# Two attention layers with one pipelined schedule: value products in pairs of quads, four probability buffers, heads divided group by group, token tiles finished in pairs

## The reference, cut to what matters

```python
def layer_a(x):                      # 16 heads of 16
    q, k, v = split(x @ Wqkv)
    q, k = rope(q), rope(k)
    q, k = q / |q|, k / |k|          # 1e-6 under the root
    a = softmax(q k^T / sqrt(16))
    return (a v) @ Wo + bo
x = layernorm(x + layer_a(x))
h = layernorm(x) * ln1_w + ln1_b
x = x + msa(h)                       # 16 heads, no rope, logits not bounded
y = layernorm(x) * ln2_w + ln2_b
x = x + expert(y)                    # 8 experts, the one with the largest gate logit
return layernorm(x + ...)            # hidden 1024, tanh gelu
```

## Time and profile before

| | us |
|---|---|
| median of 3 runs | 1553.11 (1550.62 to 1556.96) |
| the profiled execution | 1552.78, its span 1551.0 |
| busy: TensorE | 1334.5 (86%) |
| ScalarE | 959.3 (62%) |
| VectorE | 817.5 (53%) |
| GpSimd | 330.8 (21%) |

### The profile page before, as it was taken

How to read it: one execution, slowest core, us unless ns; L and a number is a source line. 1 busy time by engine, 2 the same in 40 slices (tenths; PEclk the granted TensorE clock), 3 DMA queues, 4 the chain that set the end, 5 groups by cost and what they waited for, 6 DMA issues and landing times. The chain is left out here.

```text
span 1551.0 us, 21330 instructions
## 1 busy us (share of the span) xinstructions
PE 1334.5 (86%) x7238; PEld 690.7 (45%) x7238; DVE 817.5 (53%) x1911; ACT 959.3 (62%) x1809; POOL 330.8 (21%) x337
## 2 busy tenths in 40 slices
PE   3599898898997889899999999999983499999994
PEld 1223333333332324343434343434332389899893
DVE  4232563544634267777777777777751334333341
ACT  0176776776777756666666666666670167777774
POOL 5122232322322202122212121212112201111110
PEclk9599999999999989999999999999995599999997
DMA  6212413313223312122312121212238211211113
GB/s 165 95 40 74 133 35 102 101 46 127 65 75 128 100 42 73 63 69 66 85 60 83 56 82 56 82 56 83 96 110 279 87 35 53 58 52 52 52 55 129
DMA packets 104010, 127.89 MB, mean 82 GB/s; under 512 B 7680, under 2 KB 91520, under 8 KB 103776
## 3 DMA queue, kind: packets, MB, share of 16 engines
q1 hardware_dynamic: 72080, 79.45, 16.4%
q10 hardware_dynamic: 27392, 33.56, 6.5%
q0 software_dynamic: 4432, 13.52, 2.7%
HBM read 51.51 MB, written 28.46 MB: 52 GB/s over the span
## 5 line engine op out<-in xcount | busy, mean ns | idle before, releaser
L670 ACT ACTIVATE w_space<-bank 128x512 f32<-128x512 f32 x1024 | 569.3, 600 | 296.9 <-PE bank L451 287.9
L451 PE MATMUL bank<-w_space 96*128 96x512 bf16 (+1 forms) x1024 | 366.2, 387 | 35.3 <-ACT w_space L670 21.3
L853 DVE TENSOR_REDUCE negm<-bank 128x1 f32<-128x512 f32 x512 | 327.4, 683 | 103.2 <-PE bank L478 100.2
L465 PE MATMUL bank<-w_space 128*32 128x512 f32 x2048 | 280.3, 620 | 11.4 <-ACT w_space L670 8.3
L478 PE MATMUL bank<-w_space 96*128 96x512 bf16 x512 | 198.9, 389 | 28.7 <-ACT neg_T L683 11.3
L451 PEld LDWEIGHTS bank<-w_space 96*128 96x128 bf16 (+1 forms) x1024 | 98.5, 100 | 230.0 <-ACT w_space L670 122.4
L478 PEld LDWEIGHTS bank<-w_space 96*128 96x128 bf16 x512 | 49.7, 97 | 215.4 <-DVE negm L853 104.0
L643 PE MATMUL bank<-w_space,work_space 128*128 x624 | 141.6, 380 | 0.0
L516 PE MATMUL bank<-work_space,wqkv_sb 128*128 128x512 f32 x256 | 123.3, 604 | 5.6 <-DVE w_space L973 4.8
L643 PEld LDWEIGHTS bank<-w_space,work_space 128*128 128x128 f32 x624 | 115.5, 190 | 14.3
L1242 POOL TENSOR_TENSOR row_sb<-row_sb,rows_sb 128x256 f32<-128x256 f32 x64 | 45.9, 717 | 269.9 <-DVE row_sb L1041 269.9
(11 more groups left out here) (134 smaller groups left out, 1565.4 us busy)
## 6 DMA issues: line engine op xcount, KB each, us to landing
w_space<-work_space SPq DMA_DIRECT2D x384, 128.0 KB
w_space<-in_w_dram ACTq DMA_DIRECT2D x16, 1024.0 KB, 7.9
work_space<-rows_dram SPq DMA_DIRECT2D x39, 256.5 KB, 2.6
work_space<-in_x_dram ACTq DMA_DIRECT2D x16, 512.0 KB, 4.8
x_dram<-xo SPq DMA_DIRECT2D x32, 128.0 KB, 1.7
h_dram<-row_sb SPq DMA_DIRECT2D x32, 128.0 KB, 3.6
work_space<-h_dram ACTq DMA_DIRECT2D x8, 512.0 KB, 4.1
work_space<-x_dram ACTq DMA_DIRECT2D x8, 512.0 KB, 4.7
```

Of the source, the lines that this page charges most:

```text
L451: nc.tensor.matmul(L.st_banks[c % n][:, :], k_stack[0:L.rows, s, h, kt * P:(kt + 1) * P], q_stack[0:L.rows, s, h, :], start=True, stop=Tru ...
L465: last = nc.tensor.matmul(L.pv_banks[g % n][VW * j:VW * (j + 1), :], v_aug[:, s, kt, HEADS_AT_ONCE * g + j, :], probs[:, q % 2, j, :], sta ...
L670: nc.scalar.activation(probs[:, q % 2, j, :], L.st_banks[c % len(L.st_banks)][:, :], ACT.Exp, scale=SCALE).then_inc(L.exps, 1)
L853: ve.tensor_reduce(negm[:, c % TT, c // TT:c // TT + 1], L.mx_ring.bank(use)[:, :], axis=AX.X, op=ALU.max, negate=True).then_inc(L.mx_ring ...
```

## The change

Names with heads written (q,j) are quad and head of a stage.

- **Order.** The rings and slots of `Layer` become three tables of places for single tasks, at any head; one helper, `tasks(n, q, j)`, is read by all engines. ScalarE runs the tasks of a place behind the exponential of the *next* head, in both layers. All loads of `x` move from a stage's start to its fourth quad.
- **Value products.** `pv` becomes one call for two quads, in odd quads at head 1, for quads q-3 and q-2. There are four probability buffers of a quad. The values are stored 17 columns a head instead of 32; 32 are still read.
- **PSUM.** In the first layer four banks take turns for the scores, and two for the finishing tasks; from the last first-layer batch on it is three and one. The transposes of the negated maxima move from the banks of the largest scores to the finishing bank.
- **Division.** `oT` holds one group. TO u transposes group u for all four token tiles, places (7,3), (11,3), (15,3) and (2,3) of the next stage, and VectorE divides four heads of all tiles.
- **Finishing in pairs.** TP, WO, N1, N2, HT and GT work on two token tiles. ScalarE copies 512 columns instead of 256; the roots of all four tiles are taken in one Ln and one Exp (R1, R2). GpSimd scales two tiles at once, and transfers of x1 and h1 move two tiles.
- **Last batch.** The nine weight transfers of the last stage are issued at quad 6 as before, the last of all once GT1 is done (before: once TO3 was).

What is computed, and with which passes, stays.

```diff
-            p_steps = ((1, 2, "T0"), (2, 0, "T1"), (2, 2, "qA"), (3, 2, "qB"), (4, 2, "kA"),
-                       (5, 2, "sq"), (5, 2, "kB"), (6, 2, "nq"), (7, 0, "uq"), (7, 2, "hq"),
-                       (7, 2, "sk"), (8, 2, "nk"), (8, 2, "lq"), (9, 0, "uk"), (9, 2, "hk"),
-                       (10, 0, "lk"), (10, 2, "V0"), (12, 2, "V1"))
...
-            p_steps = ((1, 2, "T0"), (2, 0, "T1"), (2, 2, "qA"), (3, 2, "qB"), (4, 0, "mq"),
-                       (4, 2, "kA"), (5, 2, "kB"), (6, 0, "mk"), (8, 2, "V0"), (12, 2, "V1"))
...
+PROJECTED = (
+    dict(T0=(0, 0), T1=(0, 2), qA=(1, 3), qB=(2, 2), kA=(3, 3), kB=(4, 2), sq=(4, 3), nq=(5, 3),
+         sk=(6, 1), uq=(6, 2), hq=(6, 3), nk=(7, 0), lq=(7, 1), uk=(8, 1), hk=(8, 2), lk=(9, 0),
+         V0=(12, 0), V1=(14, 0)),
+    dict(T0=(0, 0), T1=(0, 2), qA=(1, 2), qB=(2, 1), kA=(3, 0), mq=(3, 0), kB=(3, 3), mk=(4, 2),
+         V0=(8, 2), V1=(12, 2), NG0=(14, 2)))
+ATTENDED = (
+    dict(TO0=(7, 3), TO1=(11, 3), TO2=(15, 3)),
+    dict(NG1=(2, 1), NG2=(6, 1), TO0=(7, 3), NG3=(10, 1), TO1=(11, 3), TO2=(15, 3)))
+FINISHED = (
+    dict(TO3=(2, 3), TP0=(4, 0), TP1=(6, 3), WO0=(9, 3), WO1=(10, 2), R1=(11, 2), N10=(12, 0),
+         N11=(12, 2), R2=(13, 2), N20=(14, 0), N21=(14, 2)),
+    dict(TO3=(2, 3), TP0=(4, 0), TP1=(4, 3), WO0=(5, 3), WO1=(7, 0), R2=(8, 0), N20=(8, 2),
+         N21=(9, 0), HT0=(10, 3), GT0=(11, 1), HT1=(12, 1), GT1=(12, 3), RT=(14, 0)))
...
+        def st_bank(b, c):
+            if b < LAST_A:
+                return st_banks[c % 4], CHUNKS * b + c - 3
+            return st_banks[(CHUNKS * (b - LAST_A) + c) % 3], CHUNKS * b + c - 2
...
+            def pv(b, pair):
+                for q in (2 * pair, 2 * pair + 1):
+                    g, kt = q // TT, q % TT
+                    pe.wait_ge(exps, CHUNKS * b + HEADS_AT_ONCE * (q + 1))
+                    for j in range(HEADS_AT_ONCE):
+                        at = (kt * H + HEADS_AT_ONCE * g + j) * VS
+                        last = nc.tensor.matmul(pv_bank[VW * j:VW * (j + 1), :],
+                                                v_aug[:, b % 2, at:at + VW],
+                                                probs[:, q % PROBS, j, :],
+                                                start=(kt == 0), stop=(kt == TT - 1))
...
-                        outer_tasks((q, j - ACT_LAG[lag_of]), par, projected, finished, task)
+                        if j == 3:
+                            for b, g in group_copied(n, q):
+                                group_out(b, g)
+                        for name, b in late:
+                            task(name, b)
+                        late = tasks(n, q, j)
```

1100 lines of the change are left out of this document (538 added, 562 removed).

## The result

| | before | after |
|---|---|---|
| median | 1552.51 us (4 runs) | 1596.41 us (4 runs, 1589.58 to 1597.11) |
| ratio, 95% interval | | 1.0269 (1.0233 to 1.0304) |
| profiled execution: time, span | 1552.78, 1551.0 | 1596.25, 1594.2 |

The change makes the kernel 2.7% slower. The forecast was 1540 in a range of 1492 to 1580, with 0.31 for slower: the time lies 16 us above the range, and 5 us above what all three of its bounds make at their slow ends (1540 + 20 + 18 + 13 = 1591).

What follows compares the result with a forecast made beforehand. TensorE was taken as the engine with least slack in both layers. The terms summed as 1552.8 - 30 - 5 + 49 - 8.5 - 3 - 15 = 1540 us, in a range of 1492 to 1580.

Steps and rivals of the forecast that it cites:

- all three of its bounds: Bounds round the forecast: first layer -16 to +20 us, second layer -24 to +18, the rest -14 to +13.
- Value products in pairs: Eight pairs a stage replace sixteen single products on TensorE, each pair saving 0.2 us: 1.6 us a stage.
- First layer: Six steady first-layer stages: division wait gone, smaller waits left, 61.7 to 56.7 us each, -30 in all.
- The first stage: The stage of 56.59 us with nothing to finish: fewer waits for ScalarE, and pairs, -5 us.
- Second layer: Six steady second-layer stages: ScalarE's added delay raises waits from 7.4 to 15.1; 83 us each, +49 in all.
- Between: The two middle stages between the layers' steady ones: 66.2 and 81.3 us, together 147.5, -8.5.
- Last stage: The stage of 58.79 us before the end: pairs and no projection, -3 us.
- Tail: After the last score: transposes before the weight loads, WO0 and WO1 under them, gate result near 39 us, -15.
- The clock in the second layer: Rival: clock falls four or five times a second-layer stage; 88 us a stage, 1570 total, from about 85.5; chance 0.22.
- The range: The forecast's total range, 1492 to 1580 us, since all bounds at one end was held not likely.
- the rest: Bound for everything outside the steady stages of both layers: -14 to +13 us.

Runs made afterwards that it cites:

- e3: The changed kernel with one value product per quad again instead of pairs, all else as changed: 1541.09 us, ratio 0.9927.
- e1: The changed kernel, with ScalarE's tasks behind their own head's exponential in stages that attend in the second layer: 1548.59 us, ratio 0.9974.
- e12: The kernel before, with one number edited so ScalarE runs second-layer tasks behind the next exponential: 1594.65 us, ratio 1.0265.
- e6: The changed kernel, with the first layer's finishing at the second head of odd quads in both middle stages: 1570.94 us, ratio 1.0104.
- e9: e7, with SyncE issuing k's twelve stack-row transfers behind those of group 2's negated maxima: 1469.28 us, ratio 0.9486 to the kernel before.
- e5: The changed kernel with the edits of e1 and e3 together: 1497.62 us, ratio 0.9648 to the kernel before.
- e11: e9 with the first layer's nk one head later, at (7,1): 1460.18 us, ratio 0.9397 to the kernel before.
- e2: e1, with VectorE also running each task of those stages one largest-score tile later: 1563.69 us, ratio 1.0067 to the kernel before.
- e7: e5 plus the places of e6 in both middle stages: 1484.52 us, ratio 0.9564 to the kernel before.

## Why the prediction was wrong

- *Value products in pairs, -1.6 a stage.* The saving per pair is right (0.24 measured, 0.2 forecast), but the term is incomplete. My walk had the waits that pairs leave in even quads (qB, kB) and ahead of a pair (nk, 2.65) and booked them under the new tables, not under the pairs; that a product is also the cover of the tasks beside it was never a term. Its sign in a stage is the other one: single products are 2.5 us a stage faster (e3), in both layers.
- *First layer, -30.* The largest wait was forecast at 2.65 and is 2.63, the clock at 1.5 and is at most 1.7 (one minus the mean clock of 0.97, times a stage); the listed waits add up to 4.1, with none in quad 9, against 4.6 forecast. With the work forecast at 50.6 this leaves 1.6 us a stage that no term holds. 57.9 for 56.7, -22 for -30. The first stage fell short likewise, -1.4 for -5.
- *Second layer, +49.* Right in size (+54) and, by e1 and e12, in its main cause: ScalarE's tasks behind the next exponential cost 5.6 us a stage in the changed kernel and 6.7 in the one before. Of the rest the pairs, booked as a gain, cost 2.6. That the total came so near is in part luck: the listed waits add up to 11.5 us a stage (68.8 over the six) and not 15.1. Work forecast at 65.8, these waits and at most 2.8 of slow clock make 80.1, and 3.7 us a stage stand in no term; before, 67.4 of work and 3.9 of listed waits leave 3.5 of 74.8 likewise. The walk took the 7.4 of before for waits and replaced them whole.
- *Between, -8.5 in all.* This step failed: +17. The first stage got "waits 11.7 by the same steps, clock 1.5", the second a steady stage's waits and its 2 of clock. That left out that in these two stages VectorE still finishes the first layer, in pieces twice as long, between the second layer's reductions, and that with more waits the clock falls more often, here four times in each. The first has listed waits of 14.2 us and up to 7.0 of slow clock, the second 16.7 and up to 12.4. Moved behind products, the pieces gave back 9.6 and 10.0 us (e6 against after), some 6 and 4 of it in listed waits and the rest through the clock; with the other edits too (e9) the two stages take 64.5 and 75.0 at a clock of 1.00, under the 66.2 and 81.3 of the forecast. It was visible: the tables put N10, N11, N20 and N21 in quads 12 to 14, where these stages have the largest-score tiles, and I walked them for neither.
- *Last stage, -3.* This step failed too: +14. I priced what it lacks (a projection) and gave it neither new waits nor a clock term. It shares ScalarE's delay and the pairs with every second-layer stage: its waits are 12.5 us instead of 5.4, and its clock 0.88 instead of 1.00, worth up to 8.7. Undoing the delay takes 8.8 off (e1); e3's 3.3 for the pairs is within the scatter of this stage, but with both undone it is at 59.0 and a clock of 1.00, as before (e5), 5.0 below e1.
- *Tail, -15.* Right: -17.2.
- *The rivals.* "The clock in the second layer" had the sign, and put the mechanism in the wrong stages. Its condition, over 85.5 a steady stage by four or five falls, wasn't met: a steady stage takes 83.8 with one or two. But the two middle stages and the last have four each. In the changed kernel the stages with the most waits have the most falls, and edits that take waits away bring the clock back: 0.94 in e6's second middle stage, 1.00 in both layers' steady stages of e11. The Trainium skill's section on depth-cycling (TensorE: Matmul & The Clock Gate, A second HAM failure mode: psum-queue depth-cycling) describes such a swing by small idle gaps in another kernel, and the trace agrees in kind: 0.87 and 0.88 where the waits are most, 0.97 in the steady stages.
- *The range.* Its bound for "the rest" was 13 us either way for stages that held 42 us of surprise, and its clock terms allowed 3.5 us there for what can have cost 28. I had walked the steady stages quad by quad and the others by analogy.

Left open: what the slow clock cost exactly in the stages that missed, since the shares above are upper bounds; why one of the steady stages has more falls of the clock than the next, with the same instructions (80.0 and 86.3 us in e2); and what the choice of PSUM banks and the division by groups are worth by themselves, which no run takes apart.

## What to carry to other kernels

When two in-order engines are chained to the one that sets the pace, a small delay in the first comes back wherever work passes through both: one exponential's 0.49 us, put ahead of the nineteen tasks that ScalarE has in a stage, cost 5.6 us a stage in one kernel and 6.7 in the other. Long work on the pacing engine is cover for the others; joining two pieces saves an entry and an exit, and takes the cover from every second place. Where waits grow, price the slow clock behind them as well, stage by stage. Walk the stages that are exceptions (the first, the last, those between two phases) as carefully as the steady ones, and put a suspected cost alone into the old kernel too, which here took one number.

## What the runs showed of the hardware

GpSimd holds VectorE up. In the changed kernel a normalisation of 128x256 (L945) takes 0.41 us in the median of the 70 with no GpSimd instruction beside them and 0.99 of the 26 with one, 1.44 at most. VectorE's row below holds two norms, 1.72 us, the second of which began 0.01 us after GpSimd's:

```profile
638.58 1.72 DVE L945 TENSOR_SCALAR row_sb<-xo,mv,rstd 128x256 f32<-128x256 f32 x2
...
638.89 1.26 POOL L1221 TENSOR_TENSOR row_sb<-row_sb,rows_sb 128x512 f32<-128x512 f32 x1
```

VectorE's reductions from PSUM (L837) take 0.68 us in the median, with GpSimd beside them or not. The Trainium skill (SBUF — State Buffer, SBUF: two separate sides) says that VectorE, in a mode that takes both ports or with two inputs in SBUF, and GpSimd share a pair of ports, and that whichever starts first has it for its whole instruction. The trace agrees: the norm that started beside a GpSimd instruction of 1.26 took 1.40, and in 22 of the 26 cases the norm ended 0.15 us after the GpSimd instruction did. That is less than the 0.41 of a norm alone, so the hold ends a little before GpSimd's recorded end. The other four, beside the last 0.23 us of a GpSimd instruction or with one that started after them, took 0.40 to 0.41 as if alone. Whether VectorE slows GpSimd the runs don't show.

The traces also show that issuing in order has a price on SyncE: 0.68 us per transfer of 128 KB, 16.4 for twenty-four (e7), which a transfer of 12 KB that TensorE needed had to stand behind.
